# Routed experts: the first layer of the next expert issued ahead of the second layer of this one, weight loads split and regrouped

## The reference

```python
C = int(CAPACITY_FACTOR * T / E)              # 160
expert_idx = jnp.argmax(softmax(tokens @ gate_w.T), axis=-1)
...
dispatch = jnp.einsum('tec,td->ecd', sec_mask, tokens)
h = jax.nn.relu(jnp.einsum('ecd,edh->ech', dispatch, w1))
expert_out = jnp.einsum('ech,ehd->ecd', h, w2)
ans = jnp.einsum('tec,ecd->td', combine_weights, expert_out)
```

## Time and profile before

| | |
|---|---|
| timed executions, us | 2810.75, 2812.02, 2818.06; median 2812.02 |
| the profiled execution, us | 2816.59 |
| its span in the trace, us | 2814.5 |
| mean granted clock of TensorE over the span | 0.916 |
| busy: TensorE, VectorE, ScalarE, GpSimd, us | 2372.2, 1768.7, 935.9, 811.2 |

### The profile page before, as it was taken

The page is one execution under the profiler, slowest core; times in us unless marked ns, Lnnn a source line. Parts: engine busy times, 40 slices in busy tenths (PEclk is TensorE's granted clock), DMA queues, the critical chain, the costliest instruction groups (busy, mean ns, idle before and its releaser), DMA issues. The chain is left out here.

```text
span 2814.5 us, 35154 instructions
## 1 busy us (share of the span) xinstructions
PE 2372.2 (84%) x12910; PEld 1657.8 (59%) x12910; DVE 1768.7 (63%) x4501; ACT 935.9 (33%) x1868; POOL 811.2 (29%) x439
## 2 busy tenths in 40 slices
PE   7788888989837875977995788697998999999996
PEld 3355556436637863544653443356566788888885
DVE  5799998236524416485138993704787777766764
ACT  2498886138415201014313431131233111111110
POOL 0398884025129562001012332313001111110100
PEclk9899999999958986999997888898998999999997
DMA  2121110000135551001000000110200000000000
GB/s 90 56 66 49 49 49 16 10 0 1 39 105 171 194 163 61 1 2 37 1 19 17 1 1 0 36 38 8 112 1 5 1 1 1 1 1 1 1 1 30
DMA packets 57903, 101.08 MB, mean 36 GB/s; under 512 B 7874, under 2 KB 39362, under 8 KB 56452
## 3 DMA queue, kind: packets, MB, share of 16 engines
q1 hardware_dynamic: 56196, 94.64, 10.3%
q0 software_dynamic: 1536, 4.20, 0.5%
HBM read 88.99 MB, written 9.57 MB: 35 GB/s over the span
## 5 line engine op out<-in xcount | busy, mean ns | idle before, releaser
L749 POOL TENSOR_TENSOR XT<-mamba_DU,scan_BS 128x1024 f32<-128x1024 f32 x128 | 299.2, 2359 | 155.8 <-DMA scan_BS<-mamba_rows 118.1
L878 DVE TENSOR_TENSOR_SCAN scan_H<-scan_AB,XT 128x512 f32<-128x512 f32 x256 | 296.2, 1209 | 8.6 <-POOL XT L749 5.0
L2447 PE MATMUL ex_HP<-XT,pe_DOWN 128*128 128x256 f32 x1024 | 239.9, 389 | 11.6 <-PEq L2295 6.3
L2477 PE MATMUL ex_OP<-pe_UP,ex_GH 128*128 128x256 f32 x1024 | 241.8, 400 | 1.3 <-DVE ex_GH L2634 1.3
L2506 ACT ACTIVATE ex_GH<-ex_HP 128x512 f32<-128x512 f32 x128 | 76.3, 601 | 464.6 <-PE ex_HP L2447 337.1
L2477 PEld LDWEIGHTS ex_OP<-pe_UP,ex_GH 128*128 128x128 f32 x1024 | 205.6, 202 | 32.1 <-DVE ex_GH L2634 1.5
L2447 PEld LDWEIGHTS ex_HP<-XT,pe_DOWN 128*128 128x128 f32 x1024 | 195.2, 195 | 40.0 <-ACT ex_GH L2506 8.1
L763 PEld LDWEIGHTS scan_TP<-ident,scan_H 128*128 128x128 f32 x1024 | 120.1, 142 | 157.8 <-DVE scan_H L878 81.4
L808 ACT ACTIVATE scan_AB<-mamba_E,mamba_AA 128x510 f32<-128x510 f32 x256 | 198.7, 776 | 38.3 <-DVE scan_H L878 34.1
L772 PE MATMUL scan_YT<-mamba_BC,ident 128*128 128x512 f32 x384 | 198.4, 599 | 4.1 <-ACT scan_YS L824 2.3
L2634 DVE SCALAR_TENSOR_TENSOR ex_GH<-ex_GP,ex_GH 128x1024 f32<-128x1024 f32 x64 | 78.4, 1225 | 172.7 <-issue 154.0
(11 more groups left out here) (415 smaller groups left out, 4657.0 us busy)
## 6 DMA issues: line engine op xcount, KB each, us to landing
moe_W<-in_L_ffn_w SPq DMA_DIRECT2D x32, 1024.0 KB, 7.5
scan_BS<-mamba_rows SPq DMA_DIRECT2D x64, 256.0 KB, 3.2
pe_DOWN<-in_L_ffn_down SPq DMA_DIRECT2D x1, 4096.0 KB, 12.1
pe_UP<-in_L_ffn_up SPq DMA_DIRECT2D x1, 4096.0 KB, 22.7
moe_dispatch<-route_ZERO SPq DMA_DIRECT2D x1, 2560.0 KB, 8.8
experts_XE<-moe_dispatch SPq DMA_DIRECT2D x16, 160.0 KB, 2.4
moe_answers<-experts_YE SPq DMA_DIRECT2D x16, 160.0 KB, 3.1
XT<-in_xT SPq DMA_DIRECT2D x1, 2048.0 KB, 7.5
```

Of the source, the lines that this page charges most:

```text
L749: pool.tensor_tensor(BU[:, r % 2, cs], tokens(DU, cs, r // DS), row, ALU.mult).then_inc(bu_ready, 1)
L878: v.tensor_tensor_scan(H[:, r % 2, c], AB[:, n % 2, :], BU[:, r % 2, c], 0.0, ALU.mult, ALU.add).then_inc(h_ready, 1)
L2447: ins = pe.matmul(HP[:, n % 2, a, :], DOWN[:, k, 2 * q + a, :], XT[:, k, b * BLK:(b + 1) * BLK], start=(k == 0), stop=(k == KD - 1))
L2477: ins = pe.matmul(OP[:, m % 2, 0:D], GH[:, b % 2, j, a * P:(a + 1) * P], UP[:, j, :], start=(j == 0), stop=(j == J2 - 1))
```

## The change

The wait for weights is split into one semaphore pair for W1 and one for W2. TensorE runs the first layer of expert e+1 and turn(e+2) ahead of turn_back(e-1) and the second layer of e. ScalarE copies the answer of e-1, and VectorE copies out the answers of e-2, in the turn in which they took those of e and e-1. SP waits with XE for turn(e-2) only, with W1 for the first layer of e-2, with W2 for the second layer of e-2, and stores the answers of e-3 behind W2. Nothing is added to the arithmetic, and every transfer keeps its size.

```diff
@@ SP @@
                     if e >= 2:
-                        sp.wait_ge(y_ready, e - 1)
+                        sp.wait_ge(turned, e - 1)
                     sp.dma_start(XE[:, e % 2], dispatch[e * CAP:(e + 1) * CAP, :].rearrange("(a p) d -> p a d", p=HC_)).then_inc(x_loaded[e % 2], 16)
                     if e >= 2:
-                        sp.dma_start(W1[:, e % 2], io["L0_ffn_w1"][e].rearrange("(k p) n -> p k n", p=P)).then_inc(w_loaded[e % 2], 16)
-                        sp.dma_start(W2[:, e % 2], io["L0_ffn_w2"][e].rearrange("(k p) n -> p k n", p=P)).then_inc(w_loaded[e % 2], 16)
-                    if e >= 2:
-                        store(e - 2)
-                store(NE - 2)
-                store(NE - 1)
+                        sp.wait_ge(hid_ready, 4 * (e - 1))
+                        sp.dma_start(W1[:, e % 2], io["L0_ffn_w1"][e].rearrange("(k p) n -> p k n", p=P)).then_inc(w1_loaded[e % 2], 16)
+                        sp.wait_ge(y_ready, e - 1)
+                        sp.dma_start(W2[:, e % 2], io["L0_ffn_w2"][e].rearrange("(k p) n -> p k n", p=P)).then_inc(w2_loaded[e % 2], 16)
+                    if e >= 3:
+                        store(e - 3)
+                for e in range(NE - 3, NE):
+                    store(e)
@@ TensorE @@
-                turn(0)
-                for e in range(NE):
+                def hidden(e):
                     if e >= 2:
-                        pe.wait_ge(w_loaded[e % 2], 32 * (e // 2))
-                    else:
-                        first_loads.wait(pe)
+                        pe.wait_ge(w1_loaded[e % 2], 16 * (e // 2))
                     pe.wait_ge(turned_read, e + 1)
...
                         ins.then_inc(hid_ready, 1)
+
+                first_loads.wait(pe)
+                turn(0)
+                hidden(0)
+                turn(1)
+                for e in range(NE):
                     if e + 1 < NE:
-                        turn(e + 1)
+                        hidden(e + 1)
+                    if e + 2 < NE:
+                        turn(e + 2)
                     if e:
                         turn_back(e - 1)
+                    if e >= 2:
+                        pe.wait_ge(w2_loaded[e % 2], 16 * (e // 2))
                     pe.wait_ge(relu_act, 2 * (e + 1))
                     pe.wait_ge(relu_dve, 2 * (e + 1))
@@ ScalarE @@
+                def answer_copy(e):
+                    act.wait_ge(y_ready, e + 1)
+                    if e >= 2:
+                        act.wait_ge(y_turned, e - 1)
+                    act.activation(YS[:, e % 2].rearrange("p k n -> p (k n)"), YT[:, e % 2, 0:KD * CAP], ACT.Copy).then_inc(ys_copied, 1)
+
                 for e in range(NE):
...
                         act.activation(out, hid, ACT.Relu).then_inc(relu_act, 1)
-                    act.wait_ge(y_ready, e + 1)
-                    if e >= 2:
-                        act.wait_ge(y_turned, e - 1)
-                    act.activation(YS[:, e % 2].rearrange("p k n -> p (k n)"), YT[:, e % 2, 0:KD * CAP], ACT.Copy).then_inc(ys_copied, 1)
+                    if e:
+                        answer_copy(e - 1)
                     tables.scalar_step(act, e + 1)
+                answer_copy(NE - 1)
@@ VectorE @@
                     if e + 1 < NE:
                         take(e + 1)
-                    if e:
-                        answers_out(e - 1)
+                    if e >= 2:
+                        answers_out(e - 2)
                     if 4 <= e < 7:
                         tables.factor_step(v, e - 4)
+                answers_out(NE - 2)
                 answers_out(NE - 1)
```

More of the change, by code:

```diff
@@ L1469, in moe_experts @@
         YP = st.ps("YP", [HC_, 2, D])
-        w_loaded = [st.sem(f"w_loaded{i}") for i in range(2)]
+        w1_loaded = [st.sem(f"w1_loaded{i}") for i in range(2)]
+        w2_loaded = [st.sem(f"w2_loaded{i}") for i in range(2)]
         x_loaded = [st.sem(f"x_loaded{i}") for i in range(2)]
```

## The result

| | before | changed |
|---|---|---|
| timed executions, us | 2810.75 to 2818.06 (5), median 2814.31 | 2843.42 to 2847.35 (5), median 2844.46 |
| ratio to the kernel before | | 1.0108, 95% interval 1.0094 to 1.0122 |
| span of the profiled execution, us | 2814.5 | 2842.3 |
| mean granted clock over the span | 0.916 | 0.912 |

By the medians the changed kernel is 30.2 us slower. The forecast was 12.3 us slower, with 2834.0 as the upper end of the range; the sign and the case were right, the size was not.

A forecast was written before the change was run, and what follows sets the result against it. Experts' stage: 192.3 us, at most 39.3 to win, lost to ScalarE's relus, VectorE's factor steps and slow clock. Caught steps and 1.8 us waits move its end from 1028.2 to 1040.5, +12.3: 2812.0 + 12.3 = 2824.3 us; range 2807 to 2834.

The forecast's parts named there:

- Its case: Experts' stage: late rows, step 0 caught, no clock loss; +12.3 us, chance 0.42.
- step 0 caught: VectorE's first factor step starts after 881.98 and GpSimd's operations hold it; expert 6's first layer at 913.5.
- part (a): First layer of e+1 ahead of second layer of e: ScalarE's 17.1 us go; some 23 us offered in all.
- GpSimd's grid: Nine back-to-back GpSimd operations, 841.05 to 931.64, said to set when VectorE's factor steps 0 and 1 end.
- the edge between two cases: GpSimd's operation start at 881.98: step 0 after it is caught; before it is in time, +1.5 us, chance 0.28.
- (b): VectorE copies answers of e-2 in place of e-1; nothing waits for it, but factor steps and GpSimd's grid remain.
- (c), the size of the wait,: SP's transfer queue: XE lies behind W2 and the store, so the turn waits 1.6 to 2.1 us; 1.8 taken.
- a far bound of 2.9: Turn's wait for XE if W2 is as late as its latest, 8.8 against 7.6.
- (d), the clock,: TensorE's 1.8 us idleness costs no clock; other end 7 x 1.7 = 12 us more.
- clock falls too: Rival in the experts' stage: caught, and several slow spells; +15 to +24 us, chance 0.14.
- three signs of being wrong: XE's landing stays near 2.4, a factor step falls outside GpSimd's grid, or the clock falls in the second half.

The follow-up runs named there:

- the pair of runs with GpSimd waiting: GpSimd's third table waits for VectorE's factor steps, done in one turn: changed kernel with rows and W1 ahead, 0.9890; kernel before, old order, 0.9962.
- the faster run: Changed kernel with rows and W1 issued ahead, factor steps together in expert 7's turn, GpSimd's third table waiting for them: 2765.43 us, ratio 0.9890.
- the run with 8 filler products: Changed kernel plus 8 products on constant data, result thrown away, ahead of each of 11 turns that waited for rows: 2814.20 us, ratio 1.0072.
- the old order: For the gaps of 1.2 to 1.6: kernel before with XE(e) issued behind W1(e) instead of ahead of it; 2805.42 us, ratio 1.0037.
- the best run with the steps in shares: Changed kernel with rows and W1 issued ahead, VectorE's 25 factor instructions three to a turn, experts 4 to 12: 2780.44 us, ratio 0.9950.
- the first filler: Changed kernel plus 14 products on constant data, result thrown away, ahead of each of 11 turns that waited for rows: 2821.11 us, ratio 1.0096.

## Why the prediction was wrong in size

**Its case came true.** Rows late, step 0 caught, first layers 6 and 7 at 913.54 and 934.81 (913.5 and 934.6), expert 8 at 946.51 (945.9), so that all that part (a) offered was gone by then. That late rows and the factor steps are the causes is shown, each taken away by itself. Part of the agreement is owed to GpSimd's grid and not to the forecast: it put step 0 at 881.3 to 883.0, with 881.98 as the edge between two cases, and the same errors that made the total wrong (three waits of 7.5 us in all for 4.2 to 5.9, and two slow spells of 1.6) carried it to 889.12, clear of the edge. GpSimd's operations then let the steps go at the same times as in the forecast, so these errors didn't show up to expert 8.

**(a), (b)** held. ScalarE's 17.1 us went; the pair of runs with GpSimd waiting puts the order's worth at 16 to 20 us against the offered 23, with 7.5 us lost to the late sine in the faster run.

**(c), the size of the wait,** was 2.5 to 2.7 us in the last seven cycles, where I took 1.8, a bound of 2.1 and a far bound of 2.9. The term that was off is W2 at the head of the queue. I had bounded it by 4.7 and 5.3 us; the changed kernel's W2:

```profile
L1499 SPq DMA_DIRECT2D moe_W<-in_L_ffn_w x14: 368/390/395, 853.0 to 1042.0; - x14
...
DMA to landing us min/median/max: 5.3/5.6/6.0
```

5.6, while W1 at the head takes 5.0. XE landed 1.1 to 1.3 us behind it; 1.0 had been worked out. The 4.7 was added up from XE's landing and the spacing of W1 and W2, the 5.3 was W1's; neither was W2 at the head. The estimate by the Trainium skill ("DMA: Bandwidth & Descriptors", "Anatomy of one DMA"), a wait of 1.0 us, was further off; the fit there is of transfers issued by GpSimd, and these are SP's. Its rule of ring order ("Queues, rings and completion order") agrees with the landings: XE behind W2 and the store 5.7 us after its issue, 2.4 with the queue empty. In seven cycles: 18.0 us of waits instead of 12.6, so 5.4 more.

**(d), the clock, is the step that failed.** It said "I take none, being nearer the first": between idleness of 1.02 us that had left the clock alone and 4.13 that had lowered it, I placed 1.8 by distance, and kept 12 us as the other end. The seven cycles took 95.25 us. Less 7 x 9.56 of work and 18.0 of waits, 10.3 us are left, nearly all of it slow clock: the run with 8 filler products, which kept the clock up, puts it at 9.8. The trace of before had a nearer case that I overlooked:

```profile
913.54 6.29 PE L1552 MATMUL experts_YT<-experts_HT,moe_W 128*128 128x160 f32 x32 [3.23 <-ACT experts_HT L1569]
```

Idleness of 3.23 us had already lowered the clock there. Also, the slow spells of before cost 1.5 to 2.9 us by the starts of what follows (6.78 us from 871.59 to 878.37 against 4.42, for one), where I took 1.6 to 1.9. Had the wait been 1.8 the step might have stood: gaps of 1.2 to 1.6 did no harm in the old order, gaps of 2.24 and more did in the new. Sizing the wait 0.7 to 0.8 us short put it near gaps that do no harm. Whether 1.8 would have lowered the clock, no run shows.

The sum: 12.3 + 5.4 + 10.3, and 0.6 that was already there at expert 8, are 28.6 us, less 0.3 for an end of 14.8 us instead of 15.1; the last second layer ends 28.4 us later than before (1056.57 against 1028.2). That is the *clock falls too* case, above its +15 to +24, as its waits were longer too. The range failed since it took in only half of that case, which I gave 0.14. The forecast took one size for the wait and gave the clock a chance of its own beside it; in these runs the longer gaps are the ones with the slow clock behind them, so the two go together. Of its three signs of being wrong one came: the clock fell in the second half.

## What to carry to other kernels

When a transfer queue is served in order, look at what each transfer is put behind, and not only at what it waits for: a small transfer that is needed next goes ahead of a large one that is needed later. When TensorE gets a wait in every turn, price the clock with it, as a wait of 1.4 us cost 1.4 and one of 2.6 cost 4.1. And before giving an engine slack, see what its queue does with it: here VectorE's instructions were as long as GpSimd's operations beside them. A wait added to GpSimd was worth 25 to 30 us against the same kernel without it, and 15 to 17 against the best run with the steps in shares. It also made GpSimd's own followers late, so look at who waits for the engine that is made to wait.

## What the runs showed of the hardware that I had not expected

- Two loads of a megabyte aren't alike: W1 (rows of 4 KB) at the head of the queue landed 5.0 us after its issue, W2 (rows of 1 KB) 5.6. That the length of the rows is the reason, no run shows.
- A call of `matmul` in float32 is two instructions in the trace, and 14 calls with 160 columns took 3.97 us, 0.28 each. The "32 products" of a layer in this document are the trace's 32 instructions, from 16 calls. Taking one call for one of them halves such a cost, and that was the error in the first filler.
- VectorE's instruction over 128 x 256 with its operands in SBUF takes 0.28 to 0.43 us beside an idle GpSimd and up to 9.03 beside a busy one. The reciprocal is an exception: it took 1.75 us in both cases, as at 892.81 in the changed kernel, beside the GpSimd operation of 892.71. The Trainium skill calls the ports that the two engines share an exclusive lock ("SBUF — State Buffer", "Who interferes with whom"): whichever of the two issues first has them for the whole instruction. The rows agree in part. VectorE's first instruction, a `TENSOR_SCALAR`, did wait for the end (892.77, where GpSimd's of 882.08 ended at 892.62; the same 0.15 us behind the end in two other runs). But a `TENSOR_TENSOR` came through 9.1 us into the operations of 10.5 us of L1237 and L1238 (the one of 903.45 in the kernel before ended at 910.66, GpSimd's had begun at 901.57), and behind it up to four short ones fit in before GpSimd's next (910.90 to 912.12 in the changed kernel, GpSimd's next beginning at 912.40).
- The kernel before took 2814.3 us in one session and 2794 in the other, 0.7% apart, as much as many of the differences here. Whole times can only be compared as ratios within a session; stretches of the trace that didn't shift with the session, like the experts' stage, can be compared directly.
